# A two-layer MLP in split fp32: the order of the first transfers, transposes and matmuls is changed

## The reference

```python
h = jax.nn.gelu(jnp.einsum('bnd,hd->bnh', x, fc1_w) + fc1_b, approximate=False)
shared = jnp.einsum('bnh,sh->bns', h, fc2_w) + fc2_b
We = experts_w[indices]
be = experts_b[indices]
expert_x = jnp.einsum('bnh,bph->bnp', h, We) + be[:, None, :]
return x + jnp.concatenate([shared, expert_x], axis=-1)
```

## Time and profile before

| | us |
|---|---|
| time, median of 3 runs (lowest to highest) | 357.65 (357.59 to 357.71) |
| time of the profiled execution | 357.54 |
| its span, from the first to the last instruction | 355.4 |
| busy in the span: PE / PEld / DVE / ACT / POOL | 350.9 / 323.7 / 259.5 / 246.8 / 235.0 |

### The profile page before, as it was taken

The page is one execution under the profiler, slowest core; times in us unless marked ns, Lnnn a source line. Parts: engine busy times, 40 slices in busy tenths (PEclk is TensorE's granted clock), DMA queues, the critical chain, the costliest instruction groups (busy, mean ns, idle before and its releaser), DMA issues.

```text
span 355.4 us, 7075 instructions
## 1 busy us (share of the span) xinstructions
PE 350.9 (99%) x2381; PEld 323.7 (91%) x2381; DVE 259.5 (73%) x498; ACT 246.8 (69%) x410; POOL 235.0 (66%) x150
## 2 busy tenths in 40 slices
PE   8999999999999999999999999999999999999996
PEld 5899899999999999999999999999999999999996
DVE  2797976968859697786968869697786968844642
ACT  4885957777678577767777678577777777666560
POOL 0179887658866586865758866576865758855471
PEclk9999999999999999999999999999999999999999
DMA  8779663533333334341533324353332230312001
GB/s 239 172 162 191 140 181 85 148 99 89 112 87 117 89 90 141 94 110 59 149 98 89 114 79 122 90 137 101 84 107 64 90 99 30 120 38 89 31 30 61
DMA packets 69981, 37.53 MB, mean 106 GB/s; under 512 B 43450, under 2 KB 69946, under 8 KB 69946
## 3 DMA queue, kind: packets, MB, share of 16 engines
q1 hardware_dynamic: 69376, 36.55, 38.1%
q10 hardware_dynamic: 570, 0.53, 0.4%
HBM read 28.68 MB, written 8.39 MB: 104 GB/s over the span
## 4 chain that ended last, share of the span: by engine, by line
PE 98%; ACT 0%; issue 0%; POOL 0%; DVE 0%; POOLq 0%; ACTq 0%
PE fc_ps L1110 40%; PE acc_ps L1166 29%; PE acc_ps L1169 15%; PE fc_ps L1086 6%; PE acc_ps L1136 3%; PE acc_ps L1189 2%; PE fc_ps L1166 1%; PE fc_ps L1052 1%; PE fc_ps L1093 1%; PE fc_ps L1169 1%; PE tr_ps L1046 0%; ACT xt L461 0%; PE tr_ps L1068 0%; ACT w1t L474 0%; DVE resid L906 0%
## 5 line engine op out<-in xcount | busy, mean ns | idle before, releaser
L395 POOL TENSOR_TENSOR ht<-gelu,ht 128x1024 fp32r<-128x1024 f32 x62 | 149.5, 2411 | 97.4 <-ACT ht L565 97.4
L1166 PE MATMUL acc_ps<-w2t,ht 128*128 128x512 f32 x448 | 162.4, 397 | 0.0
L1110 PE MATMUL fc_ps<-xt,w1t 128*128 128x256 f32 x1176 | 159.9, 284 | 0.0
L1110 PEld LDWEIGHTS fc_ps<-xt,w1t 128*128 128x128 f32 x1176 | 148.7, 189 | 5.5
L1169 PE MATMUL acc_ps<-w2t,ht 128*128 128x256 f32 x448 | 125.9, 281 | 0.0
L1166 PEld LDWEIGHTS acc_ps<-w2t,ht 128*128 128x128 f32 x448 | 84.4, 188 | 14.9
L1169 PEld LDWEIGHTS acc_ps<-w2t,ht 128*128 128x128 f32 x448 | 85.0, 190 | 0.0
L565 ACT ACTIVATE ht<-gelu 128x1024 fp32r<-128x1024 f32 x64 | 68.0, 1063 | 3.6 <-issue 0.4
L591 ACT ACTIVATE gelu<-work,b 128x512 f32<-128x512 f32 x56 | 37.3, 715 | 26.2 <-DVE work L870 26.1
L403 POOL TENSOR_TENSOR xt<-work,xt 128x1024 fp32r<-128x1024 f32 x14 | 33.8, 2417 | 14.8 <-ACT xt L554 14.8
L870 DVE TENSOR_TENSOR work<-fc_ps,work 128x512 f32<-128x512 f32 x28 | 19.4, 692 | 22.6 <-PE fc_ps L1110 21.3
(11 more groups left out here) (73 smaller groups left out, 335.6 us busy)
## 6 DMA issues: line engine op xcount, KB each, us to landing
pieces<-in_L_cond_experts_w SPq DMA_DIRECT2D x128, 64.0 KB, 2.0
out<-resid SPq DMA_DIRECT2D x31, 256.0 KB, 3.1
pieces<-in_x SPq DMA_DIRECT2D x60, 128.0 KB, 2.9
resid<-in_x SPq DMA_DIRECT2D x15, 512.0 KB, 3.5
e_bias<-in_L_cond_experts_b SPq DMA_DIRECT2D x32, 32.0 KB, 2.8
work<-in_L_cond_fc_w SPq DMA_DIRECT2D x4, 256.0 KB, 4.7
w_piece<-in_L_cond_fc_w SPq DMA_DIRECT2D x4, 192.0 KB, 5.0
resid<-in_x SPq DMA_DIRECT2D x2, 256.0 KB, 3.2
```

What stands on the lines that cost most here:

```text
L395: nc.gpsimd.tensor_tensor(ht[:, slot, LO, :, :].rearrange("p k t -> p (k t)"), gelu[:, q % GELUS, :, :].rearrange("p k t -> p (k t)"), ht[ ...
L1110: last = nc.tensor.matmul(fc1_ps[:, dst, j * SEQ:(j + 1) * SEQ], w1t[:, w, wv, ms], xt[:, n % 2, o, xv, :], start=(fresh and j == 0 and at ...
L1166: nc.tensor.matmul(acc.rearrange("p (v o) -> p v o", v=2), ht[:, q % SLOTS, HI, j, ts], w2t[:, :, k, fc2_columns(b)], start=(k == 0), stop ...
```

## The change

- SP issues row 0 of x, the first half of fc1 in two DMAs of two 128-row strips each, row 1 of x, the second half of fc1, and fc2's weights, without a wait between them. ACT issues only the indices and the bias.
- The warm-ups read a tile warm_in that DVE clears as its first instruction, and wait for that; the wait for the identity comes behind them.
- Block 0's x is transposed by rows: tr_ps bank b holds row b, both d. The high and low parts are made row by row.
- PE's order becomes: warm-ups; row 0 of x; first strips of fc1 for both d; second strips; row 1 of x; bias; chunks 0 and 1 on row 0 (twelve matmuls of 256 columns); second half of fc1, now into banks 2 and 3 of fc1_ps; chunks 0 and 1 on row 1 (twelve more); chunk 2, and from there as before.
- Chunks 2 and 3 wait for the low parts of the second half of fc1, whose transposes lie in their banks; the second half of fc1 waits for the bias copy, which lies in bank 3.
- ACT: row 0, first half of fc1, row 1, second half of fc1, then the GELUs of chunks 0 and 1. DVE: the clearing, then the low parts in that order.

Context lines of the diff are left out.

```diff
@@ -90,6 +90,7 @@
+        warm_in = sbuf("warm_in", [P, P])
@@ -122,7 +123,7 @@
-        w1_loaded = [sem(f"w1_loaded{n}") for n in range(2)]
+        w1_loaded = [sem(f"w1_loaded{n}") for n in range(3)]
@@ -163,6 +164,7 @@
+        warm_ready = sem("warm_ready")
@@ -264,9 +266,20 @@
         def bank(i):
...
-        def load_w1(queue, half):
-            queue.dma_start(w1_in[:, half * HALF:(half + 1) * HALF, :], w1_halves[half])\
-                .then_inc(w1_loaded[half], 16)
+        def load_w1(queue, half, part, strips):
+            cols = slice(half * HALF + strips.start, half * HALF + strips.stop)
+            queue.dma_start(w1_in[:, cols, :], w1_halves[half][:, strips])\
+                .then_inc(w1_loaded[part], 16)
...
+        def w1_ps(half, d):
...
+            return acc_ps[:, d, :] if half == 0 else fc1_ps[:, 2 + d, :]
...
+        def x0_row(v, b):
+            return xt0[:, :, v, b * SEQ:(b + 1) * SEQ]
...
+        def x0_bank(b):
+            return tr_ps[:, b, :].rearrange("p (d t) -> p d t", d=D)
@@ -313,12 +326,14 @@
             for b in range(R):
...
-            sp.wait_ge(x0_loaded[0], 16)
-            load_w1(sp, 1)
+                if b == 0:
+                    for part in range(2):
+                        load_w1(sp, 0, part, slice(part * Q // 2, (part + 1) * Q // 2))
+            load_w1(sp, 1, 2, slice(0, Q))
@@ -374,7 +389,7 @@
-                    pool.wait_ge(x0_tr, D)
+                    pool.wait_ge(x0_tr, R)
@@ -456,10 +471,9 @@
         def _(act):
-            def x0_high(d):
-                act.wait_ge(x0_tr, d + 1)
-                nc.scalar.activation(xt0[:, d, HI, :], tr_ps[:, d, :], ACT.Copy)\
-                    .then_inc(x0_hi, 1)
+            def x0_high(b):
+                act.wait_ge(x0_tr, b + 1)
+                nc.scalar.activation(x0_row(HI, b), x0_bank(b), ACT.Copy).then_inc(x0_hi, 1)
...
             def w1_slots(half, d, v):
@@ -470,7 +484,7 @@
             def w1_high(half, d):
...
-                src = (acc_ps, tr_ps)[half][:, d, :].rearrange("p (l c) -> p l c", l=2)
+                src = w1_ps(half, d).rearrange("p (l c) -> p l c", l=2)
...
             def s_high(s):
@@ -614,7 +628,6 @@
-            load_w1(act, 0)
@@ -623,14 +636,14 @@
-            for d in range(D):
-                x0_high(d)
+            x0_high(0)
...
+            x0_high(1)
+            for d in range(D):
+                w1_high(1, d)
...
-            w1_high(1, 0)
-            w1_high(1, 1)
@@ -703,11 +716,10 @@
         def _(dve):
-            def x0_low(d):
-                dve.wait_ge(x0_hi, d + 1)
-                nc.vector.tensor_tensor(xt0[:, d, LO, :], tr_ps[:, d, :],
-                                        xt0[:, d, HI, :].bitcast(FP32), ALU.subtract)\
-                    .then_inc(x0_lo, 1)
+            def x0_low(b):
+                dve.wait_ge(x0_hi, b + 1)
+                nc.vector.tensor_tensor(x0_row(LO, b), x0_bank(b), x0_row(HI, b).bitcast(FP32),
+                                        ALU.subtract).then_inc(x0_lo, 1)
...
             def w1_slots(half, d, v):
@@ -929,12 +941,13 @@
-            for d in range(D):
-                x0_low(d)
+            nc.vector.memset(warm_in[:, :], 0.0).then_inc(warm_ready, 1)
+            x0_low(0)
...
+            x0_low(1)
@@ -945,7 +958,8 @@
-            dve.wait_ge(w1_lo, 2 * D)
...
+            dve.wait_ge(x0_lo, R)
@@ -1047,27 +1061,23 @@
             def warm(times):
-                bits = ident[:, :].bitcast(BF16)
+                bits = warm_in[:, :].bitcast(BF16)
...
             def x0_banks(b):
...
-                for d in range(D):
-                    last = transposes(tr_ps[:, d, b * SEQ:(b + 1) * SEQ],
-                                      [feature_chunk(resid[:, 0, b * T + t, :], d)
-                                       for t in range(T)])
-                    if b == R - 1:
-                        last.then_inc(x0_tr, 1)
...
-            def w1_bank(half, d):
...
-                dst = (acc_ps, tr_ps)[half][:, d, :].rearrange("p (k q c) -> p q k c", q=Q, c=S)
-                for q in range(Q):
+                transposes(tr_ps[:, b, :], [feature_chunk(resid[:, 0, b * T + t, :], d)
+                                            for d in range(D) for t in range(T)]).then_inc(x0_tr, 1)
...
+            def w1_strips(half, d, strips):
...
+                dst = w1_ps(half, d).rearrange("p (k q c) -> p q k c", q=Q, c=S)
+                for q in strips:
...
-                last.then_inc(w1_tr, 1)
+                return last
...
             def conv_operand(j, d, v):
@@ -1077,8 +1087,9 @@
             def conv_chunk(c):
...
-                if c == 3:
-                    pe.wait_ge(b1_ready, 1)
+                if 2 <= c < 4:
...
+                    pe.wait_ge(w1_lo, c + 1)
@@ -1088,19 +1099,12 @@
-            def first_chunk():
-                def product(d, w, v):
-                    return nc.tensor.matmul(fc1_ps[:, 0, :], conv_operand(0, d, w), xt0[:, d, v, :],
-                                            start=(d == 0 and w == v), stop=(d == D - 1 and w == LO))
-                for d in range(D):
-                    pe.wait_ge(w1_hi, d + 1)
-                    product(d, HI, HI)
-                    pe.wait_ge(x0_lo, d + 1)
-                    product(d, HI, LO)
-                for d in range(D):
-                    pe.wait_ge(w1_lo, d + 1)
-                    last = product(d, LO, HI)
-                last.then_inc(conv_filled, 1)
+            def first(c, b, d, w, v):
...
+                return nc.tensor.matmul(fc1_ps[:, c, b * SEQ:(b + 1) * SEQ], conv_operand(c, d, w),
+                                        xt0[:, d, v, b * SEQ:(b + 1) * SEQ],
+                                        start=(b == 0 and d == 0 and w == v), stop=True,
+                                        skip_group_check=True)
...
             def product(n, g, dst, w, o, fresh):
@@ -1195,21 +1199,46 @@
+            pe.wait_ge(warm_ready, 1)
+            warm(WARM)
...
-            warm(WARM)
-            for b in range(R):
-                x0_banks(b)
+            x0_banks(0)
...
-                w1_bank(0, d)
+                w1_strips(0, d, range(Q // 2))
+            pe.wait_ge(w1_loaded[1], 16)
+            for d in range(D):
+                w1_strips(0, d, range(Q // 2, Q)).then_inc(w1_tr, 1)
+            x0_banks(1)
...
-            first_chunk()
-            pe.wait_ge(w1_loaded[1], 16)
...
+            pe.wait_ge(x0_hi, 1)
...
-                pe.wait_ge(x0_lo, d + 1)
-                w1_bank(1, d)
-            conv_chunk(1)
+                pe.wait_ge(w1_hi, d + 1)
+                for c in range(2):
+                    first(c, 0, d, HI, HI)
+                pe.wait_ge(x0_lo, 1)
+                for c in range(2):
+                    first(c, 0, d, HI, LO)
+            for d in range(D):
+                pe.wait_ge(w1_lo, d + 1)
+                for c in range(2):
+                    first(c, 0, d, LO, HI)
+            pe.wait_ge(w1_loaded[2], 16)
...
+            pe.wait_ge(b1_ready, 1)
+            for d in range(D):
+                w1_strips(1, d, range(Q)).then_inc(w1_tr, 1)
...
+            pe.wait_ge(x0_hi, 2)
+            for c in range(2):
+                for w, v in ((HI, HI), (LO, HI), (HI, LO)):
+                    if v == LO:
+                        pe.wait_ge(x0_lo, 2)
+                    for d in range(D):
+                        last = first(c, 1, d, w, v)
+                last.then_inc(conv_filled, 1)
```

## The result

| | before | after |
|---|---|---|
| median, us (22 runs each, taken in turns) | 357.64 | 358.54 |
| lowest to highest | 357.27 to 358.81 | 357.58 to 360.35 |
| profiled execution: time / span | 357.54 / 355.4 | 359.08 / 357.0 |

The ratio is 1.0025, with a 95% interval of 1.0018 to 1.0033. The forecast was 356.3 with a range of 355.9 to 357.2: wrong in sign and in range. The profiled execution is slower than 18 of the 21 others, so its trace shows one way of being late, not all.

A forecast was written before the change was run, and what follows sets the result against it. PE was taken to bound the kernel, with 98% of the chain that ended last. Chunk 2 1.34 us earlier, less 0.09 for feeding, gave a gain of 1.25: 357.54 - 1.25 = 356.3, range 355.9 to 357.2.

The forecast's parts named there:

- What bounds the kernel: PE carries 98% of the chain, unbroken from 10.11 us; the gain is how much earlier PE reaches chunk 2.
- Warm-ups: Opening on PE: start at 1.05, 0.48 us earlier; first transpose at 3.59, clock's rise kept at 4.7.
- Transfers: Opening loads: moved bytes set the pace; row 1 lands at 5.69, fc1's second half at 7.06, fc2's weights about 10.65.
- The gap in the kernel before: SP's queue before fc1's second half, issued late at 3.51; without this gap fc2's weights land at about 10.65.
- PE in the new order: PE's opening up to chunk 2, which starts at 10.14 instead of 11.48, 1.34 us earlier.
- The check from the other side: Opening on PE: earlier start and removed waits make 1.70; less new wait, narrower matmuls and slower transposes, 1.25.
- the waits of 0.2 and 0.4: PE's waits before chunk 2 for ACT's high part and DVE's low part of fc1, claimed gone.
- What feeds PE afterwards: DVE's and POOL's chain behind fc2's weights comes forward 1.0 to 1.2, less than PE; charged 0.09.
- The slack of 0.26: POOL's low part of the first hidden pair, ending 19.04, needed by fc2 at 19.30; takes up the feeders' difference.
- C: Rival: early warm-ups fail to raise PE's clock, which rises near 9.6; cost 2.25, time 358.5; chance 0.09.
- A: Rival: transfers or DVE's chain set the pace, row 1 landing at 6.77; gain 0.2, time 357.3; chance 0.19.
- B: Rival: PE's clock rises later, between 6.4 and 9, giving 356.9 to 358.2, no change; chance 0.09.

The follow-up runs named there:

- e5: Kernel before's transfers with the change's new order and cleared warm-up tile, plus eight filler matmuls in PE's wait for fc1: 358.38 us.
- e6: Changed kernel with five more filler matmuls ahead of row 1's transposes and five ahead of fc1's second half: 358.73 us.
- e8: Changed kernel with fc1's first half in one DMA on SP's queue instead of two, twelve warm-ups: 358.56 us.
- e1: Changed kernel with SP's wait for row 0 of x put back before fc1's second half is issued: 358.43 us.
- e2: Changed kernel with fc2's weights and all behind them on SP held until row 1 of x has landed: 359.26 us.
- e10: Changed kernel with sixteen warm-ups instead of twelve: 358.15 us.
- e14: Kernel before, old order on PE, with exactly the change's transfers (fc1's first half in two DMAs on SP, no wait): 360.07 us.
- e15: Kernel before, old order on PE, without SP's wait and with fc1's first half in one DMA on SP's queue: 359.31 us.
- e17: Kernel of e8 with six warm-ups instead of twelve: 359.54 us.
- e12: Kernel before's transfers, fifteen cleared-tile warm-ups, both rows of x transposed ahead of fc1, then chunks 0 and 1 by rows: 358.24 us.
- e18: Kernel of e12 with the transposes of fc1's first half in the kernel before's order: 357.80 us.
- e4: The change's new order on PE, ACT and DVE and cleared warm-up tile, with all transfers as in the kernel before: 359.42 us.
- e9: Kernel of e8 with sixteen warm-ups instead of twelve: 357.50 us.
- e7: Kernel before with only the warm-ups changed: twelve on a cleared tile, starting at 1.06: 357.82 us.
- e11: Kernel before with only the warm-ups changed: fourteen on a cleared tile, starting at 1.06: 357.80 us.
- e3: Changed kernel with the two pieces of fc1's first half issued by ACT instead of SP, no wait on SP: 364.25 us.
- e13: Kernel before with only SP's wait for row 0 of x taken out: 358.60 us.

## Why the prediction was wrong, point by point

**What bounds the kernel** was right for this change: the span grew by what chunk 2 was delayed, 1.32, and 0.3 from late feeders. It is not the whole of it, as the 0.6 to 0.7 us that e5, e6 and e8 lost behind it show.

**Warm-ups.** The start was right (1.05 forecast, 1.06 measured). Its worth was not: I took the earlier start as a gain of 0.48 and kept the clock's rise at 4.7, which one execution had shown. The first transpose came at 3.75, 0.16 late. In the profiled execution the transposes were still at 0.21 until about 5.3.

**Transfers** is the step that failed most. I let moved bytes set the landings, each 0.6 behind the last of its bytes, and in the order of issue. In the profiled execution row 0 and the two pieces of fc1 kept to that within 0.2 (in e1, e2, e6, e10 and e14 the second piece came at 5.9 to 6.5 and not 4.97). Row 1 landed at 6.8 and not 5.69, the second half of fc1 at 10.10 and not 7.06, and the stream moved 320 GB/s where I took 361 from a stretch with two queues and larger DMAs. Two terms were missing. Two DMAs of 256 KB hold back what follows by 1.1 us against one of 512 KB (e14, e15), and transfers queued behind another take its place: 0.6 to 1.8 us for fc1's second half (e2 against e6 and the changed kernel). The gap in the kernel before, between row 1 and the second half of fc1, I priced as lost bandwidth. In it SP's queue ran empty; what it moved between 4 and 5 us:

```profile
q1 hardware_dynamic: 16, 0.01, 3.7%
```

That this kept the landings together is likely but not shown. Without such a gap the second half of fc1 landed at 8.3 to 10.1 in all kernels but two; e8 and e17 have it at 7.6 and 7.7, hardly behind the 7.5 of the kernel before. How a transfer that was nearly all moved by 7.0 came to land at 10.1 stays open.

**PE in the new order.** Some pieces of work were right: 1.43 (1.44 forecast) for twelve matmuls on row 1, no wait for DVE's low parts, none ahead of chunk 2. Others were too short: 1.69 and not 1.45 for the twelve on row 0, 1.22 and not 0.95 for eight transposes behind a wait. The check from the other side also left out 0.24 for completing the first bank of fc1 only with the sixth transpose; from e12 to e18 the difference to the kernel before fell by 0.3 with it. The main error is that I credited the order with the waits of 0.2 and 0.4 and did not compare the two orders from one landing of fc1. From there my prices add up to 5.40 (0.95 + 0.48 + 0.13 + 1.45 + 0.95 + 1.44); e4 took 5.90 for the same work, and the kernel before 5.73. Even with row 1's transposes ahead and the old strip order it is 5.66 (e18).

**What feeds PE afterwards.** fc2's weights landed near 13.4 and not 10.65, and DVE waited 0.6 for them. The slack of 0.26 that was to take up the difference was used, and PE waited 0.3 for POOL.

**The rivals.** C's 358.5 is the measured median of 358.54, but by luck: in the profiled execution the clock rose near 5.3, not at 9.6, and fc1's landing set chunk 2. A had the right mechanism with a price too small: I bounded row 1's landing at 6.77, which is what happened, but the second half of fc1, with 0.7 of slack in my sum, I did not bound by itself. C had the right mechanism, and at 0.09 too small a chance. Its rise near 9.6 is close to e8's 9.1 and e17's 9.5, but its cost of 2.25 is not borne out: e8's chunk 2 is 1.05 behind e9's, which itself waited 0.3 to 0.5 for fc1's second half. What I held against B and C, that the clock stayed high through transposes, was no evidence for a rise; I wrote so and gave it weight all the same. A and C together, not one of them, are the best account of the result: by the medians, sixteen warm-ups take 0.4 off the changed kernel (e10), one DMA in place of two another 0.65 (e9). Alone, one DMA gains nothing (e8); its trace shows the late clock and DVE's delay in place of the wait.

What stays open: how much of the changed kernel's 22 executions is clock and how much transfer, one by one, since only one has a trace; how often POOL gets ahead of DVE near 49 us; why the same transfers land up to 1.4 us apart; and why two more warm-ups took the slow end off e7 and not its median (e11).

## What to carry to other kernels

A wait that leaves a DMA queue empty for a moment may be what brings the next transfer in on time (likely here, not shown); before it is removed, bound each landing by itself, with what will be queued behind it, and not by the sum of bytes. Don't split a transfer of half a megabyte for the sake of an earlier first half when something urgent is queued behind it. Warm-ups are work with an effect: when they are moved, look at what lies between their end and the next matmuls, as e4 and e5 did. One profiled execution doesn't show how safely the clock rises, so look at the spread of many times. And compare two orders of work from the same landing before crediting one with the other's waits.

## What was not expected of the hardware

- A quarter of a megabyte on ACT's queue, behind another, took 8.4 us to land while SP's queue was full (e3); half a megabyte took 4.4 in the kernel before. The second queue gave no priority.
- The same kernel with six, twelve and sixteen warm-ups: 359.54, 358.56, 357.50. The clock's rise was seen between 3.8 (e2) and 16.5 us (e3).
- Taking one wait out of the kernel before put five of twelve executions above 359.8 (e13); of the 35 of the kernel before beside it, two were.
- One DVE subtraction took 0.42 us when it began at most 6 ns behind an instruction of POOL, and 1.28 when it began 8 ns behind (e5, e6, e8). That moved the span by 0.6 to 0.7.
